# Four score banks instead of two inside the MLP block, all of the next unit's first 24 score pairs in it, and Q and K of its second half made earlier

## What is computed

```python
# stage 0 (keys from ctx, mask per batch row), stage 1 (keys from ctx), stage 2 (keys from x, one mask),
# stage 3 (causal, keys from x), stage 4 (keys from ctx): 16 heads of 16 features
h = layer_norm(x)
q, k, v = h @ wq, keys @ wk, keys @ wv
attn = softmax(where(mask, -inf, q @ k.T * 16 ** -0.5))       # 512 x 512 for each head
x = x + (attn @ v) @ wo
# after stages 0, 2 and 4
x = x + gelu(layer_norm(x) @ w1 + b1) @ w2                    # hidden size 1024
# last attention: 16 heads of 64 features, RMS norm, no MLP
```

## Time and profile before

| | us |
|---|---|
| three runs, median (lowest to highest) | 4929.38 (4928.25 to 4931.38) |
| the profiled execution | 4919.61 |
| its span, first to last instruction | 4917.8 |
| PE busy in it | 4589.4 (93%) |
| DVE busy | 2994.1 (61%) |
| ACT busy | 2304.8 (47%) |
| POOL busy | 1062.8 (22%) |

### The profile page before, as it was taken

The page is one execution under the profiler, slowest core; times in us unless marked ns, Lnnn a source line. Parts: engine busy times, 40 slices in busy tenths (PEclk is TensorE's granted clock), DMA queues, the critical chain, the costliest instruction groups (busy, mean ns, idle before and its releaser), DMA issues.

```text
span 4917.8 us, 66126 instructions
## 1 busy us (share of the span) xinstructions
PE 4589.4 (93%) x24369; PEld 1861.1 (38%) x24484; DVE 2994.1 (61%) x7970; ACT 2304.8 (47%) x3011; POOL 1062.8 (22%) x991
## 2 busy tenths in 40 slices
PE   6999999989998999999899989999989999999999
PEld 2333343433333333343444433343333333333334
DVE  6777776656668777676466675555524455454554
ACT  4455554466665444444455554444433334333333
POOL 0112221111111111111121111111113333333333
PEclk9999999999999999999999999999999999999999
DMA  1111111121121111011111211111110000000000
GB/s 61 35 50 56 51 42 43 35 91 55 61 67 52 37 39 34 31 35 49 66 62 62 74 63 47 38 35 49 40 65 22 13 1 13 13 13 13 1 13 9
DMA packets 164513, 201.67 MB, mean 41 GB/s; under 512 B 36321, under 2 KB 119649, under 8 KB 162914
## 3 DMA queue, kind: packets, MB, share of 16 engines
q1 hardware_dynamic: 141154, 176.34, 10.7%
q0 software_dynamic: 23040, 21.10, 1.7%
HBM read 128.86 MB, written 68.42 MB: 40 GB/s over the span
## 4 chain that ended last, share of the span: by engine, by line
PE 58%; issue 20%; DVE 13%; ACT 5%; DMA 2%; POOL 1%; SPq 0%; DVEq 0%; POOLq 0%; ACTq 0%
PE psO L725 7%; PE small L654 7%; PE small L661 6%; PE psT L700 5%; PE psT L930 5%; PE psS L682 4%; PE psT L783 3%; DVE nmb L1191 3%; ACT probs L1011 3%; PE psT L654 2%; PE psT L890 2%; PE psO L945 2%; PE psT L945 2%; PE psT L900 2%; DVE nmb L1188 2%
## 5 line engine op out<-in xcount | busy, mean ns | idle before, releaser
L1011 ACT ACTIVATE probs<-psT 128x1024 f32<-128x1024 f32 (+3 forms) x1280 | 1160.0, 961 | 1226.0 <-PE psT L700 1049.5
L1191 DVE TENSOR_REDUCE nmb<-psS 128x1 bf16<-128x512 f32 x1024 | 650.2, 684 | 347.5 <-PE psS L682 347.2
L1188 DVE CUSTOM_DVE_ANT_0 out<-psS,pens_sb 128x512 f32<-128x512 f32 x1024 | 666.2, 685 | 268.8 <-issue 267.5
L700 PE MATMUL psT<-low 32*128 32x512 f32 (+3 forms) x5120 | 735.1, 595 | 25.7 <-ACT probs L1011 22.8
L682 PE MATMUL psS<-out 32*128 32x512 bf16 (+3 forms) x2560 | 590.0, 374 | 111.3 <-DVE nmb L1188 50.0
L725 PE MATMUL psO<-probs,V 128*32 128x512 f32 (+3 forms) x5120 | 653.9, 583 | 9.2 <-DVE probs L1200 7.6
L1374 DVE TENSOR_REDUCE parts<-psS 128x2 bf16<-128x1024 f32 x256 | 314.9, 1230 | 531.3 <-PE psS L917 531.3
L1117 ACT ACTIVATE probs<-psT 128x1024 f32<-128x1024 f32 x256 | 262.2, 1024 | 524.9 <-PE psT L933 524.9
L682 PEld LDWEIGHTS psS<-out 32*128 32x128 bf16 x2560 | 149.5, 91 | 807.0 <-issue 440.7
L783 PE MATMUL psT<-out,W 128*128 128x512 f32 x768 | 382.9, 620 | 0.4
L1522 POOL TENSOR_TENSOR oN<-oN,probs 128x1024 f32<-128x1024 f32 x128 | 300.7, 2350 | 316.0 <-ACT probs L1117 315.6
(11 more groups left out here) (184 smaller groups left out, 5644.3 us busy)
## 6 DMA issues: line engine op xcount, KB each, us to landing
o_mid<-out SPq DMA_DIRECT2D x160, 256.0 KB, 2.0
oN<-o_mid POOLq DMA_DIRECT2D x160, 128.0 KB, 3.5
oN<-r_mid SPq DMA_DIRECT2D x80, 256.0 KB
x_mid<-xe SPq DMA_DIRECT2D x40, 512.0 KB, 2.9
xw<-x_mid SPq DMA_DIRECT2D x36, 512.0 KB, 4.1
xe<-x_mid SPq DMA_DIRECT2D x36, 512.0 KB, 5.0
cT<-ctxT SPq DMA_DIRECT2D x20, 512.0 KB, 5.1
W<-wm SPq DMA_DIRECT2D x6, 1024.0 KB, 8.3
```

What stands on the lines that cost most here:

```text
L700: last = nc.tensor.matmul(psT[j][:, q0:S], Kf[rows_of(j), q, a, c, kt * P:(kt + 1) * P], Qf[rows_of(j), q, a, c, q0:S], start=True, stop=p ...
L1011: nc.scalar.activation(probs[:, i % 2, two, q0:S], psT_all[:, two, q0:S], ACT.Exp, scale=float(DH) ** -0.5)\
L1188: nc.vector.tensor_tensor_reduce(junk[:, e, 0:n], psS[e][:, 0:n], penalty, 1.0, -3.0e38, ALU.add, ALU.max, at).then_inc(sem[f"s_read{e}"], 1)
L1191: nc.vector.tensor_reduce(at, psS[e][:, 0:n], AX, ALU.max).then_inc(sem[f"s_read{e}"], 1)
```

## The change

The block is widened. For i = 0, 1, 2 ... `max_scores_in_block` puts both halves of step i (a **four**: heads j = 2, 3, 0, 1) behind one slot: the first half into `psS[0]`, `psS[1]` as before, the second into `psT[2]`, `psT[3]` (`block_bank`). The second half's matmuls wait until DVE has read the second half of the four before. In the 20 bodies that make 24 pairs ahead there are 12 fours, none behind slots 0, 4, 8 and 12 and one behind each other slot; the pairs in steps 12 to 15 are gone. In the two bodies with 16 pairs ahead there are 8 fours, one behind each odd slot. The last MLP bodies, without a `nxt`, have none.

`from_hidden` writes `psT[0]` in place of `psT[2]`. `exp_scores` of step 10, which writes all of `psT`, now also waits until DVE has read every four (`s_read0`, `s_read1`). DVE's `take_hidden(0)` stands behind maximum pair 18 of 24 (before: 12 of 16).

Since pairs 16 to 23 need c = 1, the fill q1 moves from slot 21 (late in step 10) to slot 11 (late in step 5) and k1 from slot 23 (late in step 11) to slot 17 (late in step 8).

```diff
-NXT_USES = {True: uses_at("6 x0, 7 x1, 9 q0, 16 k0, 21 q1, 23 k1, 25 m0, 27 v0, 29 v1"),
+NXT_USES = {True: uses_at("6 x0, 7 x1, 9 q0, 11 q1, 16 k0, 17 k1, 25 m0, 27 v0, 29 v1"),
...
     if mlp:
-        last = [(0, 1, 1)] + 3 * [(1, 1, 0)] if out > IN_BLOCK else 4 * [(0, 0, 0)]
-        return [(0, 0, 0)] + 8 * [(1, 0, 0)] + 3 * [(0, 0, 0)] + last
+        return [(0, 0, 0)] + 8 * [(1, 0, 0)] + 7 * [(0, 0, 0)]
...
+        def block_bank(k, e):
+            return psT[2 + e] if k else psS[e]
+        def z_bank(nxt):
+            return psT[2] if nxt is None else psT[0]
...
+            def max_scores_in_block(place, u, i):
...
+                for k in range(2):
+                    for e in range(2):
+                        j = 2 * (1 - k) + e
+                        if i or k == 0:
+                            pe.wait_ge(sem[f"s_read{e}"], count(f"s_read{e}", u, 2 * i - (1 - k if i else 0)))
+                        nc.tensor.matmul(block_bank(k, e)[:, 0:n], Qb[rows_of(j), q, a, c, qt * P:(qt + 1) * P], Kb[rows_of(j), q, c, 0:n],
+                                         start=True, stop=True).then_inc(sem[f"s_full{e}"], 1)
...
-                dst = psT[2] if t < 2 else small[:]
+                dst = z_bank(nxt) if t < 2 else small[:]
...
                 def maximum_next(n):
-                    if nxt is not None:
-                        max_scores(place, nxt, n // 2, n % 2, True)
+                    slots = FC + 2 * T
+                    quads = place.body.out // 2 if nxt is not None else 0
+                    for i in range(n * quads // slots, (n + 1) * quads // slots):
+                        max_scores_in_block(place, nxt, i)
...
                             pe.wait_ge(sem["z_read"], count("z_read", prev, 1))
+                            for e in range(2 if nxt is not None else 0):
+                                pe.wait_ge(sem[f"s_read{e}"], count(f"s_read{e}", nxt, place.body.out))
                         exp_scores(place, cur, i)
...
-                for n in range(IN_BLOCK):
+                for n in range(place.body.out):
                     if nxt is not None:
-                        maximum(nxt, n // 2, n % 2)
+                        maximum(nxt, n // 2, n % 2, [block_bank(n % 2, e) for e in range(2)])
...
-                    if n == 3 * IN_BLOCK // 4:
+                    if n == 3 * place.body.out // 4:
```

More of the change, by code:

```diff
@@ L148, in maxima @@
             if self.mlp and i == MLP_AFTER:
-                n += IN_BLOCK
+                n += self.out
         return steps
@@ L683, in max_scores @@
                                      start=True, stop=True).then_inc(sem[f"s_full{e}"], 1)
+            def max_scores_in_block(place, u, i):
+                g, qt = divmod(i, T)
+                c, a, q = g // 2, g % 2, u.parity
+                n = (qt + 1) * P if u.s == CAUSAL else S
+                if qt == 0 and a == 0:
+                    wait_taken(pe, place, "nxt", place.last("nxt", f"k{c}"))
+                    pe.wait_ge(sem["q_low"], count("q_low", u, c + 1))
+                for k in range(2):
[5 more added lines that the diff above has]
+                                         start=True, stop=True).then_inc(sem[f"s_full{e}"], 1)
             def exp_scores(place, u, i):
@@ L784, in hidden, with from_hidden @@
                 last.then_inc(sem["f_full"], 1)
-            def from_hidden(place, u, t, part):
+            def from_hidden(place, u, t, part, nxt):
                 if t == 0 and part == 0:
                     pe.wait_ge(sem["f_read"], count("f_read", u, FC))
-                dst = psT[2] if t < 2 else small[:]
+                dst = z_bank(nxt) if t < 2 else small[:]
                 for m in range(FC // 2 * part, FC // 2 * (part + 1)):
@@ L815, in mlp @@
                     for part in range(2):
-                        from_hidden(place, u, t, part)
+                        from_hidden(place, u, t, part, nxt)
                         maximum_next(FC + 2 * t + part)
@@ L1171, in normalise, with maximum @@
                 return last
-            def maximum(u, i, k):
+            def maximum(u, i, k, banks=psS):
                 g, qt = divmod(i, T)
@@ L1187, in maximum @@
                         nc.vector.memset(scratch[:, 6 + e:7 + e], 0.0)
-                        nc.vector.tensor_tensor_reduce(junk[:, e, 0:n], psS[e][:, 0:n], penalty, 1.0, -3.0e38,
+                        nc.vector.tensor_tensor_reduce(junk[:, e, 0:n], banks[e][:, 0:n], penalty, 1.0, -3.0e38,
                                                        ALU.add, ALU.max, at).then_inc(sem[f"s_read{e}"], 1)
                     else:
-                        nc.vector.tensor_reduce(at, psS[e][:, 0:n], AX, ALU.max).then_inc(sem[f"s_read{e}"], 1)
+                        nc.vector.tensor_reduce(at, banks[e][:, 0:n], AX, ALU.max).then_inc(sem[f"s_read{e}"], 1)
             def limit(u, i):
@@ L1252, in reciprocals, with take_hidden @@
                 nc.vector.tensor_tensor(rsum[:, 0, :], rsum[:, 1, :], valid64[:], ALU.mult).then_inc(sem["recip"], 1)
-            def take_hidden(place, u, k):
-                src = (psT[2], small[:])[k]
+            def take_hidden(place, u, k, nxt):
+                src = (z_bank(nxt), small[:])[k]
                 if k == 0:
@@ L1311, in mlp @@
                     limit(cur, MLP_AFTER)
-                for n in range(IN_BLOCK):
+                for n in range(place.body.out):
                     if nxt is not None:
-                        maximum(nxt, n // 2, n % 2)
+                        maximum(nxt, n // 2, n % 2, [block_bank(n % 2, e) for e in range(2)])
                     if cur is None and n <= T:
                         tail_maximum(n)
-                    if n == 3 * IN_BLOCK // 4:
-                        take_hidden(place, u, 0)
-                take_hidden(place, u, 1)
+                    if n == 3 * place.body.out // 4:
+                        take_hidden(place, u, 0, nxt)
+                take_hidden(place, u, 1, nxt)
             def body(place, prev, cur, nxt):
```

1 line of the change is left out of this document (removed).

## The result

The changed kernel takes 5014.24 us (median, 5008.95 to 5018.34) against 4928.82 for the kernel before beside it: a ratio of 1.0173, 95% interval 1.0155 to 1.019. It is slower by 85 us; 4998 was forecast.

A forecast was written before the change was run, and what follows sets the result against it. PE, busy 93% of the span, was taken to bound the kernel. Body terms summing to +52 us and +17 us for the clock, added to 4929.4, gave 4998 us; range 4945 to 5050.

The forecast's parts named there:

- Fewer changes of row size: In the block, 12 fours replace 16 pairs at 0.475 us of PE each: -1.9 us a body.
- Waits in the block: PE waits inside the block for DVE, which needs 2.48 us a four against a 2.24 us slot: +4.4 us a body.
- The wait at the end: After the last four, step 10's scores wait until DVE has read psT[2] and psT[3]: +3.0 us a body.
- Parts 1 to 3: The block and the wait behind it together, less 0.4 us for the last pair: +5.1 us a body.
- Steps 10 to 15: Behind the block, steps without q1, k1 and 8 pairs fall towards ACT's floor: -7.6 us in stage 0, -8.5 in stage 4.
- q1: Fill moved to step 5, behind y01; costs PE's own work, with ACT's take hidden: +1.9 us a body.
- k1: Fill moved to step 8; waits 1.1 us for ACT's take of k0 and delays step 9's exponentials: +3.5 us a body.
- POOL and SP, "nothing": POOL's copy of c = 1 can run before slot 2 and SP's order is unchanged: no cost.
- The clock: PE's clock drops behind the wait at the block's end in half of 22 bodies, 1.6 us each: +17 us.
- Rival A: In the block and at its end, DVE is never waited for and the clock's term goes: 4836 us, chance 0.08.
- B: k1 costs only PE's work (+1.9 us) and the block's waits are half: 4897 us (4940 with half of that), chance 0.16.
- C: The clock falls in every body, once or twice, 37 or 75 us in place of 17: 5018 to 5056 us, chance 0.22.

## Why the prediction was right, point by point

1. *Fewer changes of row size* (-1.9 us a body): right. A four costs 0.49 us where 0.475 was taken.
2. *Waits in the block* (4.4 us): right in place and order. The first is 0.92 us where 0.8 was taken; with the third four's 0.23 the block up to the last four is 39.3 us long (760.72 to 800.01), where the working gives 38.8.
3. *The wait at the end* (3.0 us): 3.25 us. Parts 1 to 3 together were put at +5.1 and are +5.8 in stage 0, +5.2 in stage 4. The difference in stage 0 is the 0.25 us here and 0.5 us in the block.
4. *Steps 10 to 15*: -7.9 where -7.6 was forecast, in the stage 0 bodies with full clock. They are at ACT's floor, as said: 806.41 - 803.26 = 3.15 us. In stage 4 they lost 6.0 to 7.3 us where 8.5 was forecast; with PE kept at work in the wait they take 19.2 us there, the forecast's 19.3, so the difference is the clock's.
5. *q1*: +1.91, forecast +1.9.
6. *k1*: +3.7, forecast +3.5; 1.03 us of wait for k0's take where 1.1 was worked out. The block starts 10.05 us behind k0 (750.67 to 760.72), forecast 9.9.
7. *POOL and SP, "nothing"*: this was wrong in a few bodies. y01 in step 5 waits for POOL's scaling of the attention's output, whose data come by DMA. Behind the sixth block, and behind the second wide block of stage 4:

```profile
848.30 2.31 PE L666 MATMUL small<-Wo,oN 128*128 128x256 f32 x7 [3.94 <-POOL oN L1501]
3238.66 3.65 PE L666 MATMUL small<-Wo,oN 128*128 128x256 f32 x8 [2.01 <-POOL oN L1501]
```

   The first had a wait in the kernel before too, of 2.05 us, so this one is 1.9 us longer; the second had 0.27 us, ended by ACT. In the second, y01 also runs at half clock, 3.65 us where the row of before has 1.96, and the two together are most of what steps 5 to 7 lose there above the 1.9 that was due (+5.6). That is part of why stage 4 lost 3.4 to 7.5 us a body and not 2. Why POOL's data came later was not tried.
8. *The clock*: forecast +17 us; the estimate from the kernel that keeps PE at work is 17 to 20. The cause is right, the agreement in size is partly luck. Half clock stands behind the wait in 17 of 22 bodies, not in half of them, and costs 24.0 us in the 16 that can be compared, 1.5 a body where 1.6 was taken; and the 33 us of half clock that these steps already had before were not set against it. The two errors nearly cancel.

The sum: measured +85, forecast +69. With the clock at 17 in both, the rest is 68 where 52 was forecast; 0.7 us a body in the block of the masked stages make some 10 of the 16 us, and the waits for POOL are among what remains. The moves and the banks can't be told apart to the microsecond: the moves alone cost 0.87% and the whole change 1.73%, each with its own half clock inside. At full clock, in a body of stage 0, the moves are 2.1 us and the banks the other 1.5 of the 3.6. Rival A (DVE never waited for) fell in the block's first three fours; its price was rounded loosely in the prediction, 145 us where 7 us in 20 bodies are 140 and the terms' 7.4 would be 148, which changes no chance. B (partly hidden) fell with k1, +3.7 and not +1.9, and with waits in the block that were whole. C has the number of bodies more nearly right than the forecast, and the measured 5014 lies 4 us below its lower end and 16 above the forecast.

## What to carry to other kernels

A cheaper way of issuing the same work is only worth what the reader behind it can take: compute the reader's time for one batch (here 4 x 0.62 us) against the interval at which batches come, and put nothing that overwrites the banks directly behind the last batch. Batches twice as far apart, fewer of them, and the fills left in place turned a loss of 1.7% into one of 0.2%; moving the same batches by one slot, so that work stands behind the last, made a gain of 1.7% of it, with the same banks. Work that is moved to make room has to be costed through every hop of its new place, its single bank and the order of the engine that empties it.

## What the runs showed that was not expected

- A wait of 3 us on PE costs more than itself: with full steps behind it, half clock came twice in each of six bodies and cost 5.3 us (steps 10 to 15 of stage 0, 26.7 to 32.0 us), and three matmuls of no use in the wait made the kernel 56 us faster. In a kernel whose steps behind the wait have slack on PE, the same cure brought 24 us. Behind a wait of 0.9 us it brought nothing that can be told. Five of the changed kernel's 22 bodies have the same 3 us wait and no half clock behind it; why is open.
- The three matmuls cost next to no time: the scores started 42.62 us behind the block's start with them, 42.54 without.
